# Decoder layer on one core: feed-forward tokens parted 384 + 512 instead of 448 + 448, second layer norm parted alike, weighted values copied mostly by ScalarE, instruction lists in another order

## The reference

```python
x = _layernorm(x + attention(x))          # 16 heads, low-rank queries, shared latent keys/values, rotary part, causal
x = _layernorm(x + cross_attention(x, ctx_512))   # 16 heads of 32; causal, so only the first 112 of 375 context rows count
x = _layernorm(x + feed_forward(x))       # 2 shared experts of 2048 hidden + top 2 of 16 routed experts of 128 hidden
```

## Time and profile before

| | |
|---|---|
| runs | 837.65, 836.65, 836.73 us; median 836.73 |
| profiled execution, its own time | 836.77 us |
| its span, first to last instruction | 835.2 us |
| granted TensorE clock, mean over the span | 0.997 |
| PE busy | 812.3 us (97%) |
| VectorE busy | 551.6 us (66%) |
| ScalarE busy | 458.1 us (55%) |
| GpSimd busy | 244.2 us (29%) |

### The profile page before, as it was taken

One profiled execution on the slowest core, in us unless ns is written; L12 is line 12 of the kernel. 1 busy time (PEld: TensorE's weight loads), 2 busy tenths in 40 slices (PEclk: granted clock), 3 DMA queues, 4 the chain that ended last, 5 costly groups with the idle time before them and its releaser, 6 DMA issues.

```text
span 835.2 us, 13390 instructions
## 1 busy us (share of the span) xinstructions
PE 812.3 (97%) x4238; PEld 694.8 (83%) x4238; DVE 551.6 (66%) x1026; ACT 458.1 (55%) x1187; POOL 244.2 (29%) x284
## 2 busy tenths in 40 slices
PE   7999999999999999999979999999999999999997
PEld 5887888888888888787858788888889888888885
DVE  4657755854865778899997565355655656656466
ACT  6427544643743667877876524344746637557050
POOL 0142320331222141655553005312332322320510
PEclk9999999999999999999999999999999999999999
DMA  9213323151261153412220306334654645634522
GB/s 340 77 45 114 147 88 80 57 208 44 69 226 42 42 180 96 95 39 55 57 72 1 101 5 234 140 126 140 192 182 170 227 144 177 217 120 139 143 72 89
DMA packets 42894, 100.06 MB, mean 120 GB/s; under 512 B 16160, under 2 KB 24224, under 8 KB 41728
## 3 DMA queue, kind: packets, MB, share of 16 engines
q1 hardware_dynamic: 31792, 61.67, 23.2%
q0 software_dynamic: 11056, 37.79, 13.9%
HBM read 71.65 MB, written 20.97 MB: 111 GB/s over the span
## 4 chain that ended last, share of the span: by engine, by line
PE 84%; DVE 6%; issue 4%; ACT 3%; POOL 3%; DMA 0%; DVEq 0%; POOLq 0%
PE ps L1562 68%; PE ps L1719 3%; PE ps L1903 2%; PE ps L1583 2%; PE ps L1617 2%; PE ps L1893 2%; ACT Pt L888 1%; PE ps L1727 1%; POOL Pt L645 1%; DVE sT L1150 1%; DVE acc L1176 1%; PE ps L1905 1%; PE ps L1788 1%; DVE PT_lo L1092 1%; DVE zf L1325 1%
## 5 line engine op out<-in xcount | busy, mean ns | idle before, releaser
L645 POOL TENSOR_TENSOR Pt<-Pt,rowinv 112x448 f32<-112x448 f32 x64 | 62.5, 980 | 193.9 <-DVE rowinv L1166 193.4
L1562 PE MATMUL ps<-x2T_hi,ws_hi 128*128 128x448 f32 x256 | 95.3, 372 | 0.4 <-DVE x2T_lo L1092 0.4
L1562 PE MATMUL ps<-x2T_hi,ws_lo 128*128 128x448 f32 x256 | 93.7, 366 | 0.0
L1562 PE MATMUL ps<-x2T_lo,ws_hi 128*128 128x448 f32 x256 | 93.7, 366 | 0.0
L1562 PE MATMUL ps<-w_hi,h_hi 128*128 128x512 f32 x224 | 90.0, 402 | 0.0
L1019 ACT ACTIVATE hf<-ps,b 128x448 f32<-128x448 f32 x64 | 40.6, 634 | 88.0 <-PE ps L1562 87.4
L1562 PE MATMUL ps<-w_hi,h_lo 128*128 128x512 f32 x224 | 88.5, 395 | 0.0
L1562 PE MATMUL ps<-w_lo,h_hi 128*128 128x512 f32 x224 | 88.5, 395 | 0.0
L1448 DVE TENSOR_TENSOR acc<-ps,acc 128x512 f32<-128x512 f32 x56 | 38.6, 689 | 45.0 <-PE ps L1562 45.0
L1092 DVE TENSOR_TENSOR h_lo<-hf,h_hi 128x448 fp32r<-128x448 f32 x64 | 39.8, 624 | 41.2 <-ACT h_hi L1020 41.1
L769 POOL DMA_INDIRECT wg<-in_wtab,ix_i x29 | 31.0, 1068 | 108.6 <-DVE ix_i L1433 57.8
(11 more groups left out here) (289 smaller groups left out, 2266.5 us busy)
## 6 DMA issues: line engine op xcount, KB each, us to landing
stage<-in_wf SPq DMA_DIRECT2D x30, 513.0 KB, 4.0
rows_in<-in_zeros SPq DMA_DIRECT2D x30, 256.0 KB, 5.4
xs<-rows_in POOLq DMA_DIRECT2D x29, 256.0 KB, 4.2
rows_out<-yb POOLq DMA_DIRECT2D x29, 256.0 KB, 2.6
stage<-in_wb SPq DMA_DIRECT2D x4, 1280.0 KB, 5.8
stage<-in_wa SPq DMA_DIRECT2D x8, 512.0 KB, 4.3
qr<-ro_hi SPq DMA_DIRECT2D x64, 56.0 KB, 2.0
qr<-ro_lo SPq DMA_DIRECT2D x64, 56.0 KB, 1.9
```

The costliest lines, as they stand in the source:

```text
L645: nc.gpsimd.tensor_tensor(p, p, rowinv[0:S, b % 2, :].unsqueeze(2).broadcast_to([S, GH, S]), ALU.mult).then_inc(norm_done, 1)
L1562: ins = mm(dst, w, x, start=start and i == 0, stop=stop and i == len(ops) - 1, skip_group_check=not (start and stop))
```

## The change

1. `UP_TILES`: the two token halves of the feed-forward become 3 tiles (384 columns) and 4 tiles (512 columns), in the products, the gelus, the `h_lo` subtractions and the router's logits.
2. `LN_PARTS[1]` becomes tiles 0 to 2 and 3 to 6, and the first product waits for three turned tiles.
3. `zf` copies: in pairs ACT takes heads 0, 1, 2 and DVE head 3; of single sequences ACT takes all four and DVE none (its list item does nothing).
4. New orders in all the `ATT_LAST`, `X_PRE`, `X` and `X_LAST` lists; the attention loop's lists stay as they are. In `ATT_LAST`, POOL has `LK` ahead of `N` 4, `KZ` behind `CX` and `L` behind `N` 6, and `K` 0 comes behind `Z` 6 on PE, ACT and DVE. In `X` and `X_LAST`, DVE takes `N` earlier against its neighbours, `N` 7 now ahead of `Z` 5 among them.

```diff
+UP_TILES = [(0, 3), (3, TT)]
+UP_COLS = [slice(P * lo, P * hi) for lo, hi in UP_TILES]
+UP_N = [P * (hi - lo) for lo, hi in UP_TILES]
-LN_PARTS = [[(0, 4), (4, 6), (6, TT)], [(0, 4), (4, TT)]]
+LN_PARTS = [[(0, 4), (4, 6), (6, TT)], [(0, 3), (3, TT)]]
...
# X_LAST_PE, from ("W", 3) on
-    ("W", 3), ("T", 7), ("Z", 6), ("W", 4), ("Z", 7), ("U2", 0), ("U2", 1), ("U2", 2), ("U2", 3), ("W", 5),
-    ("W", 6), ("FF", 0), ("FF", 1), ("FF", 2), ("U2", 4), ("U2", 5), ("U2", 6), ("FF", 3)]
+    ("W", 3), ("T", 7), ("Z", 6), ("Z", 7), ("U2", 0), ("W", 4), ("U2", 1), ("W", 5), ("U2", 2), ("W", 6),
+    ("FF", 0), ("FF", 1), ("U2", 3), ("U2", 4), ("U2", 5), ("FF", 2), ("U2", 6), ("FF", 3)]
# X_LAST_ACT, from ("ROOT2", 0) on
-    ("ROOT2", 0), ("Z", 6), ("ROW2", 0), ("ROW2", 1), ("U2", 0), ("Z", 7), ("U2", 1), ("U2", 2), ("U2", 3),
-    ("ROOT2", 1), ("FF", 0), ("ROW2", 4), ("ROW2", 5), ("U2", 4), ("U2", 5), ("U2", 6), ("FF", 1), ("FF", 2), ("FF", 3)]
+    ("ROOT2", 0), ("Z", 6), ("ROW2", 0), ("ROW2", 1), ("U2", 0), ("Z", 7), ("U2", 1), ("U2", 2), ("ROOT2", 1),
+    ("ROW2", 4), ("ROW2", 5), ("U2", 3), ("FF", 0), ("U2", 4), ("U2", 5), ("U2", 6), ("FF", 1), ("FF", 2), ("FF", 3)]
# X_LAST_DVE, from ("Z", 5) on
-    ("Z", 5), ("N", 7), ("W", 3), ("T", 6), ("STAT2", 2), ("STAT2", 3), ("VAR2", 0), ("T", 7), ("ROOT2", 0),
-    ("ROW2", 2), ("Z", 6), ("Z", 7), ("W", 4), ("ROW2", 3), ("U2", 0), ("U2", 1), ("U2", 2), ("U2", 3), ("W", 5),
-    ("W", 6), ("STAT2", 4), ("STAT2", 5), ("STAT2", 6), ("VAR2", 1), ("ROOT2", 1), ("ROW2", 6), ("U2", 4),
+    ("N", 7), ("Z", 5), ("T", 6), ("W", 3), ("STAT2", 2), ("STAT2", 3), ("VAR2", 0), ("T", 7), ("Z", 6),
+    ("ROOT2", 0), ("ROW2", 2), ("W", 4), ("U2", 0), ("Z", 7), ("W", 5), ("U2", 1), ("U2", 2), ("STAT2", 4),
+    ("W", 6), ("STAT2", 5), ("STAT2", 6), ("VAR2", 1), ("ROOT2", 1), ("ROW2", 3), ("ROW2", 6), ("U2", 3),
...
# X_POOL
-    (NEXT, "LK"), ("N", 4), (NEXT, "L"), ("N", 5), ("X",), ("Z", 1), ("N", 6), ("N", 7), ("Z", 3), (NEXT, "N", 0),
-    (NEXT, "N", 1), ("Z", 5), ("Z", 7), (NEXT, "N", 2), (NEXT, "N", 3)]
+    (NEXT, "LK"), ("N", 4), (NEXT, "L"), ("Z", 1), ("X",), ("N", 5), ("N", 6), ("N", 7), ("Z", 3), (NEXT, "N", 0),
+    ("Z", 5), (NEXT, "N", 1), ("Z", 7), (NEXT, "N", 2), (NEXT, "N", 3)]
...
+        Z_ON_ACT = 3
...
# ACT, x_step, kind "Z"
-                    for h, dst, src in heads_apart(j, not alone(g, j)):
-                        if h < 2:
-                            ins = copy(dst, src)
-                    ins.then_inc(z_hi, 1 if alone(g, j) else 2)
+                    if alone(g, j):
+                        for h, dst, src in heads_apart(j, False):
+                            ins = copy(dst, src)
+                            if h == 1:
+                                ins.then_inc(z_hi, 1)
+                        ins.then_inc(z_free, 1)
+                    else:
+                        for h, dst, src in heads_apart(j, True):
+                            if h < Z_ON_ACT:
+                                ins = copy(dst, src)
+                        ins.then_inc(z_hi, 2)
# PE, up_half
-                    pe.wait_ge(lt_lo, TT + (4, TT)[half])
-                product(ps[:, q % 3, 0:HALF],
+                    pe.wait_ge(lt_lo, TT + UP_TILES[half][1])
+                product(ps[:, q % 3, 0:UP_N[half]],
# PE, down_tile
-                pe.wait_ge(h_lo_done, 4 + 2 * FG * n + (FG if (t + 1) * P <= HALF else 2 * FG))
+                pe.wait_ge(h_lo_done, 4 + 2 * FG * n + (FG if t < UP_TILES[0][1] else 2 * FG))
```

More of the change, by code:

```diff
@@ L207 @@
+X_PRE_POOL = [("F", 0), ("F", 1), ("N", 0), ("N", 1), ("N", 2), ("N", 3)]
 X_PE = [
[L208 to L211, removed]
@@ L212 @@
-    ("W", 6)]
+    ("S", 5), ("Z", 1), ("T", 3), ("S", 6), (NEXT, "K", 0), ("Z", 2), ("T", 4), ("S", 7), (NEXT, "Q", 0),
+    (NEXT, "K", 1), ("Z", 3), ("T", 5), (NEXT, "V", 0), ("Z", 4), (NEXT, "S", 0), (NEXT, "S", 1), ("Z", 5), ("T", 6),
+    (NEXT, "S", 2), ("W", 0), ("T", 7), (NEXT, "Q", 1), ("Z", 6), ("W", 1), (NEXT, "T", 0), (NEXT, "S", 3), ("Z", 7),
+    ("W", 2), ("W", 3), (NEXT, "T", 1), (NEXT, "S", 4), ("W", 4), (NEXT, "V", 1), (NEXT, "Z", 0), (NEXT, "T", 2),
+    ("W", 5), ("W", 6)]
@@ L217 @@
+    (NEXT, "S", 1), (NEXT, "Q", 1), (NEXT, "T", 0), (NEXT, "S", 2), ("Z", 7), (NEXT, "T", 1), (NEXT, "S", 3),
     (NEXT, "V", 1), (NEXT, "T", 2)]
 X_DVE = [
[L219 to L221 removed]
@@ L222 @@
-    (NEXT, "S", 3), ("Z", 7), ("W", 2), ("W", 3), (NEXT, "T", 0), (NEXT, "N", 2), ("W", 4), (NEXT, "S", 4),
+    ("T", 2), ("N", 4), ("Z", 1), ("S", 5), ("T", 3), ("S", 6), ("N", 5), (NEXT, "K", 0), ("S", 7), (NEXT, "Q", 0),
+    ("Z", 3), ("T", 4), ("T", 5), ("N", 6), (NEXT, "K", 1), ("N", 7), (NEXT, "S", 0), (NEXT, "V", 0), (NEXT, "S", 1),
+    ("T", 6), ("W", 0), (NEXT, "N", 0), ("Z", 5), (NEXT, "S", 2), ("T", 7), (NEXT, "Q", 1), (NEXT, "N", 1), ("W", 1),
+    (NEXT, "S", 3), ("W", 2), ("Z", 7), ("W", 3), (NEXT, "N", 2), (NEXT, "T", 0), ("W", 4), (NEXT, "S", 4),
@@ L428, in build @@
         h_hi, h_lo = pair("h", [P, FG, T])
-        hf = sb("hf", [P, 4, HALF])
+        hf = sb("hf", [P, 4, max(UP_N)])
         b1g = sb("b1g", [P, 2])
@@ L1013, in up_half @@
                 q = 2 * FG * n + FG * half + j
-                cols = slice(half * HALF, (half + 1) * HALF)
+                cols, n_cols = UP_COLS[half], UP_N[half]
                 act.wait_ge(up_done, q + 1)
@@ L1018, in up_half @@
                 bias = b1[:, j:j + 1]
-                nc.scalar.activation(hf[:, q % 4, :], ps[:, q % 3, 0:HALF], ACT.Gelu, bias=bias)
-                nc.scalar.activation(h_hi[:, j, cols], ps[:, q % 3, 0:HALF], ACT.Gelu, bias=bias)\
+                nc.scalar.activation(hf[:, q % 4, 0:n_cols], ps[:, q % 3, 0:n_cols], ACT.Gelu, bias=bias)
+                nc.scalar.activation(h_hi[:, j, cols], ps[:, q % 3, 0:n_cols], ACT.Gelu, bias=bias)\
                     .then_inc(gelu_done, 1)
@@ L1319, in x_step @@
                     transposed(m + j, j)
-                elif kind == "Z" and (j % 2 or alone(g, j)):
+                elif kind == "Z" and j % 2 and not alone(g, j):
                     dve.wait_ge(z_done, m + j + 1)
                     dve.wait_ge(zs_lo, B * g + j + 1)
-                    for h, dst, src in heads_apart(j, not alone(g, j)):
-                        if h >= 2:
+                    for h, dst, src in heads_apart(j, True):
+                        if h >= Z_ON_ACT:
                             ins = nc.vector.tensor_copy(dst, src)
-                    ins.then_inc(z_free, 1 if alone(g, j) else 2)
+                    ins.then_inc(z_free, 2)
                 elif kind == "W":
@@ L1437, in up_half @@
                 q = 2 * FG * n + FG * half + j
-                cols = slice(half * HALF, (half + 1) * HALF)
+                cols = UP_COLS[half]
                 dve.wait_ge(gelu_done, q + 4)
-                low(h_lo[:, j, cols], hf[:, q % 4, :], h_hi[:, j, cols]).then_inc(h_lo_done, 1)
+                low(h_lo[:, j, cols], hf[:, q % 4, 0:UP_N[half]], h_hi[:, j, cols]).then_inc(h_lo_done, 1)
             def down_tile(n, t):
@@ L1509, in unit_step @@
                         dve.wait_ge(g_log, half + 1)
-                        V.tensor_copy(lg[:, half * HALF:(half + 1) * HALF],
-                                      ps[0:2 * E, 5 + half, 0:HALF]).then_inc(g_lg, 1)
+                        V.tensor_copy(lg[:, UP_COLS[half]], ps[0:2 * E, 5 + half, 0:UP_N[half]]).then_inc(g_lg, 1)
                 elif (n, k) == (0, 7):
@@ L1813, in logits @@
                 for k in range(KD):
-                    x = two((x2T_hi, x2T_lo), slice(None), k, slice(half * HALF, (half + 1) * HALF))
+                    x = two((x2T_hi, x2T_lo), slice(None), k, UP_COLS[half])
                     for i, part in enumerate(x):
-                        ins = mm(ps[0:2 * E, 5 + half, 0:HALF], gw_hl[:, k, :], part, start=k == 0 and i == 0,
+                        ins = mm(ps[0:2 * E, 5 + half, 0:UP_N[half]], gw_hl[:, k, :], part, start=k == 0 and i == 0,
                                  stop=k == KD - 1 and i == 1)
@@ L1853, in up_half @@
                 if n == 0 and j == 0:
-                    pe.wait_ge(lt_lo, TT + (4, TT)[half])
-                product(ps[:, q % 3, 0:HALF],
+                    pe.wait_ge(lt_lo, TT + UP_TILES[half][1])
+                product(ps[:, q % 3, 0:UP_N[half]],
                         [(two(ws, slice(None), slice(D * j + P * k, D * j + P * k + P)),
-                          two((x2T_hi, x2T_lo), slice(None), k, slice(half * HALF, (half + 1) * HALF)))
+                          two((x2T_hi, x2T_lo), slice(None), k, UP_COLS[half]))
                          for k in range(KD)]).then_inc(up_done, 1)
```

25 lines of the change are left out of this document (11 added, 14 removed), and 52 rows, old and new, of tables (ATT_LAST_ACT, ATT_LAST_DVE, ATT_LAST_PE, X_LAST_ACT).

## The result

The changed kernel takes 840.01 us (median of 7 runs, 838.95 to 840.49), the kernel before it 837.13 us (836.58 to 837.99) beside it: ratio 1.0031, 95% interval 1.0022 to 1.0041. It is **slower by 0.3%**, where 831.7 was predicted with a range of 828.8 to 835.0. Its profiled execution took 840.01 us, span 838.4.

A forecast was written before the change was run, and what follows sets the result against it. PE was taken to have the most work, with loop turns also limited by a chain over DVE and ACT; -2.1 - 0.4 - 3.5 + 1.0 = -5.0 gave 831.7 us, 8-in-10 range 828.8 to 835.0.

The forecast's parts named there:

- The feed-forward costed as unchanged: Feed-forward split 384 + 512: matmul cost in proportion to columns, 32 products of either width, so 0.
- Loop, -2.1: Three cross-attention loop turns: one pair copy moved from DVE to ACT gains 0.7 us a turn, ends 0 and -5.7.
- rival A: Loop does not get shorter, limited by the exp, `N`, `T`, `Z` round trip over four engines: 833.8 us, chance 0.20.
- Rival D: ACT becomes the loop's bound, four copies lengthening every turn by 1.36 us: 838.3 us, chance 0.07.
- End of attention and opening, -0.4: End of attention and opening of cross attention: new orders alone win PE idle time, -0.4 us, ends -1.5 and +0.5.
- The spreading of the keys, costed at nothing: SP's key spreading, touched by moved `KZ` and `K` 0: no cost, since cross-attention scores come many microseconds behind `K` 0.
- Last group, -3.5: Up to the first feed-forward product: DVE's queue shortened by copies and norm work moved away, -3.5 us, ends -5.5 and -1.
- rival B: Last-group boundary does not move: last sequence's chain, with four ACT copies in a row, ends as late: 835.2 us, chance 0.09.
- Behind the first product, +1.0: After the first feed-forward product, PE waits for ACT's longer chain of norm rows and gelus: +1.0 us, ends 0 and +2.
- Rival C: Feed-forward's 384-column matmuls held to the weight load's 188 ns, +5.1 us: 836.8 us, chance 0.03.

The follow-up runs named there:

- experiment 12: Changed kernel with a 0.86 us POOL fill behind each tile's two scatters, spacing them out: 835.94 us, ratio 0.9992.
- experiment 7: Kernel before (448 + 448) with scatters about 0.5 us earlier, the second weight gather moved behind them and two fills ahead: 843.47 us, ratio 1.0075.
- experiment 11: Changed kernel with its 14 indirect scatters replaced by plain stores of the same bytes to fixed rows, so without the routing: 837.94 us.
- Experiment 3: Changed kernel with 448 + 448, norm parts and last-group lists of before; changed opening and loop lists and all copies on ACT kept: 836.42 us, ratio 0.9995.
- experiment 8: Kernel before with only the changed loop lists and three of four pair copies on ACT: 834.44 us, ratio 0.9969.
- Experiment 9: Kernel before with only the pair copies changed, three on ACT and one on DVE, all lists as before: 837.92 us, ratio 1.0012.
- experiment 10: Kernel before with only the changed loop lists of the four engines, copies two and two: 834.34 us, ratio 0.9972.
- experiment 6: Changed kernel with one GpSimd fill of 0.49 us ahead of the scatters: 843.93 us, ratio 1.0074.
- experiment 5: Changed kernel with the zf copies two on ACT and two on DVE as before, lists, split and norm parts changed: 840.82 us, ratio 1.0047.

## Why the prediction was wrong, step by step

The forecast was 8.3 us too low (840.0 against 831.7), and two steps failed. One is the feed-forward, costed as unchanged: 4.3 us. The other is the last group together with the end of attention and the opening, put at -3.9 and measured at +0.65: 4.5 us. Either alone puts the time outside the range: without the stall it is 835.94 (experiment 12), still above 835.0, and the forecast with the stall alone would be 836.0. The ends of the prediction's terms add up to 824.0 and 838.2, so even these don't hold 840.0; none of its rivals is the stall.

**The feed-forward costed as unchanged: this is the first step that failed.** It said "32 products of either width: 0" and expected the stretch from the first product to the end "as long as before, or 1 us longer". It is 5.1 us longer. The arithmetic of the split was right (0.175 us a matmul; split alone with spaced scatters, last experiment: 0.6 us in all, spent behind the first product). What it left out is a moved step: the first half ends sooner, and with it the DVE steps that compute the rows' places, and POOL's 14 scatters, which run beside turn 1's output tiles. I costed the split on PE, ACT and DVE, and did not ask what POOL was doing in the same turn. The price was 4.26 us. The wait of PE for nobody in the earlier trace rows was true of one arrangement only: experiment 7 shows the kernel before losing 6.5 us in that stretch from a POOL shift alone.

Shown: the stall occurs with indirect scatters one behind the other (in six executions); spacing took it away in four of four runs, plain stores in two of two; and it needs neither the split (experiment 7) nor heavy traffic (experiment 11). Spacing and plain stores also shift the moments of the scatters, so what exactly they change is not isolated.

Five other kernels send dense scatters and have no stall (before, and experiments 3, 8, 9, 10). The traces hold something that parts the two groups. In all five the fourth scatter keeps POOL for 2.0 us; in all six executions with the stall no scatter takes more than 1.3. So the later ten scatters come some 1.3 us sooner against the output tiles where the stall occurs: the last one starts 13.3 us behind the end of output tile 0 in all six, 14.6 in the five. The spacing of 0.49 us brings that to 15.1. This orders all cases that experiment 6 left unordered, but no run was made to test it, and it does not say why. Nor are the five all free of late signals: experiments 3 and 8 have one, with scatters placed as in the kernel before, and it happens not to hold PE. (The trace has lost a few records of signals in experiments 3, 5 and 8; the late start of DVE's addition is the firmer evidence there.) What makes the fourth scatter longer, and what inside the chip holds PE's signal back for up to 7.5 us, could not be seen. That cause stays open.

**Loop, -2.1: right in size, wrong in mechanism.** Measured -2.5 (0.7 in the first turn, 0.9 in each of the others). I priced it by DVE's relief from one copy a pair. Experiment 9 makes that relief and the turn stays at 28.17 us, which is what rival A said of the copies; experiment 10 leaves the copies and gets 27.10. The gain is the order's, so that the size came out is luck. My own reading had the pieces: PE's need of 26.1 us and a chain that wandered over four engines said that order could bring up to 1.9 us a turn; I then tied it to a load count. Rival D (ACT becomes the loop's bound) fell, though ACT is busy 24.78 of 27.97.

**End of attention and opening, -0.4: wrong.** Measured +0.5 to +0.6 in every kernel with the changed lists of this part; without them (experiments 8 and 10) it is 0.0. The step that failed is where I looked: I counted PE's idle time from 306.00 to 334.68 and expected an order to win some of it. In that stretch the idle time did vanish (28.68 of 28.68), but the new lists lose some 0.4 us ahead of it, in `ATT_LAST`, where an output product now waits for DVE, and as much behind it, at the entry of the loop. Which of the moved items does it was not tested. The spreading of the keys, costed at nothing, is not what I can show as the loss: PE waits 0.8 us for the keys' second half at 335.9 us, but the scores that wait start no later than in the kernel before.

**Last group, -3.5: wrong, and the second step that failed.** The last piece went from 23.08 to 23.13 us in the changed kernel. Among seven executions of its lists and copies it is 23.0 to 23.1 in three, with a mean clock of 0.94 from 418.62 to 446.60, and 23.6 to 23.8 in four, with 0.88. None gains. The failed reading is "ACT has 8 us to spare in this stretch". DVE's queue did shrink, but ACT's spare time lay elsewhere in the stretch; where the last sequences finish, the rows of four copies (twelve of the sixteen, 0.25 us each), exp and a table load stand one behind the other for 8 us on the path. Experiment 3 beside 8 puts a price on it: with the old order, moving the single copies to ACT makes the last piece 1.1 us longer (24.15 for 23.02, though at a granted clock of 1.00 where experiment 8 has 0.94). The new order wins that back and no more. The four copies in a row on ACT are rival B's mechanism, to which I had given 0.09. The order and the copies belong together, though: with the new order and the copies back on DVE (experiment 5) F comes 1.4 to 2.3 us later than with both.

**Behind the first product, +1.0:** measured +0.69, within its ends, but mostly for another reason. 0.44 of it is PE's own work, the four transposes of tile 3 that moved behind F (I had counted DVE's and ACT's share of the moved tile, not PE's); ahead of the first 512-column product, where I expected the wait for ACT's gelus, PE's starts show a gap of 0.37 us where 0.175 is regular, 0.2 us.

**Rival C** (384 columns held to 188 ns) is refuted by the 0.175. The Trainium skill, "TensorE: Matmul & The Clock Gate", section on LDWEIGHTS, gives the load less time than such a matmul takes; by that rule the spacing is free, and the trace agrees.

**The sum, by what was measured:** +0.6 (end of attention and opening) - 2.5 (loop) + 0.05 (last piece) + 0.7 + 4.3 + 0.1 (behind the stall) = +3.2, the span's +3.2. Without the stall the change would have been worth about 1 us (experiment 12 beside the kernel before: 1.2 us from 837.13, 1.0 from 836.96, the median measured with it), not 5.0. The best kernel found keeps only its loop lists: 834.34 us, 0.28% faster than before.

## What to carry to other kernels

When a change lets one step end sooner, list what the idle-looking engines and queues do in that turn, and hold the new moments against each other; "PE never waits here" describes one arrangement. Where indirect scatters from GpSimd have time to spare and another engine's signals come late beside them, try spacing them out: here 3.4 us of fills among 14 of them cost nothing that shows and removed 4.3 us. Before pricing a gain by work taken off a busy engine, try the new order with the old work and the new work with the old order; and read an engine's spare time where the chain runs, not over the stretch.

## What the runs showed of the hardware

- PE's completion signal came 1.1 to 7.5 us late while GpSimd sent indirect scatters back to back (about 1.3 us from start to start), in the changed kernel at a DMA share of 0.4 to 0.9. Plain stores of the same rows, at a share of 1.0 and 418 GB/s, did not delay it.
- A single idle time of 2.5 us of PE was followed by a granted clock of 0.66 in the mean over the next 5 us, so that the stall of 2.5 us cost 4.3. In experiment 5 PE waited 2.0 us at the same place, the granted clock stayed at 1.00, and the stretch was 2.7 us longer.
- An indirect scatter of 128 rows of 2 KB keeps POOL for 1.0 us, now and then for up to 2.0, a plain store of as many bytes for 0.55 us.
- The kernel's first 1000 matmuls, the same in all kernels, were through between 196.2 and 198.1 us after the start of the execution; that spread of 1.8 us is nearly as large as the one between the runs of a kernel (837.7 to 835.7 for the kernel before in one set of 22).
